# Layer 1 of a two-layer transformer: the opening stage's order of work on five queues, and the experts' products in one-pass float32r parts

## What is computed

```python
# end of layer 0 and opening of layer 1
h = jnp.tanh(jnp.einsum('tbi,oi->tbo', x, wo) + c_final @ uo.T + bo)   # z and cu hold the two summands
x = x + h
q = _layernorm(x, axis=-1) @ W_q.T + b_q
# experts of layer 1: E = 8, K = 2, hidden width 1024
h = jax.nn.gelu(jnp.einsum('ecd,edh->ech', buf, W1) + b1[:, None, :], approximate=False)
y = jnp.einsum('ech,ehd->ecd', h, W2) + b2[:, None, :]
```

## Time and profile before

| what | value |
|---|---|
| median of 3 runs | 6165.45 us (6163.56 to 6171.82) |
| the profiled execution, its own time | 6167.23 us |
| its span in the trace | 6165.5 us |
| mean granted TensorE clock | 0.91 |
| open_full, first DMA issue to the next stage's first | 1574.1 to 1814.5 us |
| experts, first DMA issue to the next stage's first | 4946.2 to 5977.5 us |

### The profile page before, as it was taken

One profiled execution on the slowest core, in us unless ns is written; L12 is line 12 of the kernel. 1 busy time (PEld: TensorE's weight loads), 2 busy tenths in 40 slices (PEclk: granted clock), 3 DMA queues, 4 the chain that ended last, 5 costly groups with the idle time before them and its releaser, 6 DMA issues. The chain is left out here.

```text
span 6165.5 us, 88753 instructions
## 1 busy us (share of the span) xinstructions
PE 5124.5 (83%) x27631; PEld 2717.2 (44%) x27632; DVE 3176.9 (52%) x6296; ACT 2503.8 (41%) x3173; POOL 1018.8 (17%) x786
## 2 busy tenths in 40 slices
PE   6778996699458999999999999999964089999970
PEld 3435664444224444443444444444343056666650
DVE  4556763211337888887888788888734000000013
ACT  1223552112114777776776677777620011111110
POOL 3440002311330000000000000000023700000016
PEclk8888998899778999999999999999876589999985
DMA  6445665700565333333333333333154421111115
GB/s 216 121 119 156 164 164 164 217 24 24 141 174 78 61 62 61 67 67 66 67 67 67 55 51 62 62 67 57 28 159 149 139 69 65 52 52 49 56 58 183
DMA packets 363364, 579.30 MB, mean 94 GB/s; under 512 B 56576, under 2 KB 258751, under 8 KB 360816
## 3 DMA queue, kind: packets, MB, share of 16 engines
q1 hardware_dynamic: 344976, 523.46, 35.7%
q0 software_dynamic: 14768, 50.51, 2.3%
q10 hardware_dynamic: 3264, 0.79, 0.1%
HBM read 297.72 MB, written 197.24 MB: 80 GB/s over the span
## 5 line engine op out<-in xcount | busy, mean ns | idle before, releaser
L1180 DVE TENSOR_REDUCE full_peak<-full_item 128x1 f32<-128x512 f32 (+2 forms) x3392 | 2036.2, 655 | 481.0 <-PE full_item L1247 475.4
L1150 ACT ACTIVATE full_prob<-full_score 128x1024 f32<-128x1024 f32 (+1 forms) x1792 | 1649.9, 960 | 659.9 <-PE full_score L1258 653.6
L1247 PE MATMUL full_item<-full_kst,full_qst 49*128 49x512 f32 (+1 forms) x4096 | 1205.2, 407 | 55.3 <-DVE full_peak L1180 23.8
L1258 PE MATMUL full_score<-full_qst,full_kst 51*128 51x512 f32 (+1 forms) x3328 | 1112.8, 448 | 17.3 <-ACT full_prob L1150 11.9
L1258 PEld LDWEIGHTS full_score<-full_qst,full_kst 51*128 51x128 f32 (+1 forms) x3328 | 481.1, 183 | 932.2 <-ACT full_prob L1150 600.6
L1272 PE MATMUL full_value<-full_prob,full_vaug 128*17 128x512 f32 x6656 | 887.0, 605 | 0.8 <-ACT full_raw L1137 0.7
L1247 PEld LDWEIGHTS full_item<-full_kst,full_qst 49*128 49x128 f32 x4096 | 630.5, 189 | 200.3 <-DVE full_peak L1180 129.4
L2069 ACT ACTIVATE moe_hT<-moe_hbank,moe_b 128x512 f32<-128x512 f32 (+1 forms) x320 | 199.4, 623 | 806.6 <-PE moe_hbank L2124 802.1
L2136 PE MATMUL moe_ybank<-moe_w,moe_hT 128*128 128x256 f32 x2176 | 485.1, 384 | 5.2 <-ACT moe_hT L2069 5.2
L2124 PE MATMUL moe_hbank<-moe_xT,moe_w 128*128 128x512 f32 (+1 forms) x1280 | 477.5, 531 | 6.4 <-DMA moe_b<-in_b 6.4
L2136 PEld LDWEIGHTS moe_ybank<-moe_w,moe_hT 128*128 128x128 f32 x2176 | 414.7, 192 | 67.3 <-issue 6.0
(11 more groups left out here) (207 smaller groups left out, 5282.2 us busy)
## 6 DMA issues: line engine op xcount, KB each, us to landing
full_kst<-full_high SPq DMA_DIRECT2D x256, 200.1 KB
full_ctxT<-in_ctxT SPq DMA_DIRECT2D x16, 1601.0 KB, 9.1
full_kst<-full_low SPq DMA_DIRECT2D x128, 200.1 KB
win_qst<-scratch_q SPq DMA_DIRECT2D x384, 64.0 KB, 2.6
full_qst<-scratch_q SPq DMA_DIRECT2D x384, 64.0 KB
scratch_xbuf<-ctxp_zero POOLq DMA_DIRECT2D x17, 1024.0 KB
scratch_attn<-win_raw SPq DMA_DIRECT2D x64, 256.0 KB, 2.1
scratch_q<-open_parts SPq DMA_DIRECT2D x128, 128.0 KB, 2.3
```

Source lines behind the costliest of these rows:

```text
L1150: nc.scalar.activation(prob[h][(s.par * PAIRS + t) % 2][0:rows, 0:banks, :], score[u % 2][0:rows, 0:banks, :], ACT.Exp, scale=SCALE).then_ ...
L1180: nc.vector.tensor_reduce(peak[s.par][:, hq:hq + len(qts), c], src, AX, ALU.max).then_inc(item_read, 1)
L1247: ins = nc.tensor.matmul(ps[:, at:at + z - a], qst[s.slot][rows, h // 2, qt * P:(qt + 1) * P].bitcast(F32R), kst[s.slot][rows, h // 2, a:z ...
L1258: ins = nc.tensor.matmul(score[u % 2][0:z - a, kt % 2, :], kst[s.slot][rows, h // 2, a:z].bitcast(F32R), qst[s.slot][rows, h // 2, :].bitc ...
```

## The change

In open_full: z, x1 and x2 get four buffers and semaphores of their own, and SP loads four batches ahead. The loops are written out. POOL adds cu two batches ahead (the z adds of 0 and 1 first; then for each n: the power, the z add of n+2, the low parts of n-1). ACT takes over the bias (`whole`) from DVE, and runs tanh of n+1, the copies and the bias reads of n. DVE runs for each n: the add, the statistics, the high parts of n-1, the centring of n. A pair of q stores becomes one, four stores a batch.

In experts: every operand of the two products is split into a high part (low 12 bits masked off) and a low part (the difference), both of type float32r, and each product becomes high by high, high by low and low by high. The hidden block takes 3 matmuls for each of its two halves. In the output rows the high part of h multiplies W2's high and low parts side by side (512 columns, halves of one PSUM bank), and the low part of h multiplies W2's high part (256 columns). DVE splits the weights of the next expert in eight pieces (three in chunk 1, three in chunk 2, two in chunk 3; those of expert 0 ahead of everything), the turned rows out of PSUM, and the hidden blocks; ACT makes the float32r copy of the hidden block's high part; DVE adds the two halves of an output bank and the bias, in two instructions for each tile. Rows are loaded two chunks ahead, and the raw weights have one buffer.

```diff
@@ open_full
+    BUFS = 4
...
         @block.gpsimd
...
-            def early(n, par):
-                pool.wait_ge(loads_in[par], 32 + 16 * (n - par))
-                nc.gpsimd.tensor_tensor(z[par][:, :, :], z[par][:, :, :], cu[:, :, :], ALU.add).then_inc(pre_done, 1)
-                pool.wait_ge(var_done, n + 1)
-                nc.gpsimd.tensor_tensor(norm[3][:, :], norm[2][:, :], minus_half[:, :], ALU.pow).then_inc(rstd_done, 1)
...
+            add_state(0)
+            add_state(1)
+            for n in range(BATCH):
+                pool.wait_ge(var_done, n + 1)
+                nc.gpsimd.tensor_tensor(rstd[:, :], var_eps[:, :], minus_half[:, :], ALU.pow).then_inc(rstd_done, 1)
+                if n + 2 < BATCH:
+                    add_state(n + 2)
+                if n > 0:
+                    low_parts(n - 1)
+            low_parts(BATCH - 1)
...
         @block.scalar
...
+            def read_queries(n):
+                for c in range(KC):
+                    act.wait_ge(q_full, KC * n + c + 1)
+                    if n >= 2:
+                        act.wait_ge(low_done, KC * (n - 2) + c + 1)
+                    nc.scalar.activation(whole[n % 2][c][:, :], qbank[2 * (n % 2) + c][:, :], ACT.Identity,
+                                         bias=bq[:, c:c + 1]).then_inc(q_read, 1)
...
         @block.vector
...
+            for n in range(BATCH):
+                add(n)
+                measure(n)
+                if n > 0:
+                    high_parts(n - 1)
+                centre(n)
+            high_parts(BATCH - 1)
@@ experts, ACT
+            def high_hidden(n, c, k):
+                cols = (CHUNKS[c][1] - CHUNKS[c][0]) * P
+                act.wait_ge(h_cut_done, (n * NC + c) * HC + k + 1)
+                nc.scalar.copy(h_high[:, k, 0:cols], h_cut[k % RING][:, 0:cols]).then_inc(h_high_done, 1)
...
-                        nc.scalar.activation(hT[parity(par, c)][:, k, 0:cols], hbank[k % 4][:, 0:cols], ACT.Gelu,
+                        if not (isinstance(n, int) and n == 0 and c == 0 and k < RING):
+                            act.wait_ge(h_low_done, (n * NC + c) * HC + k + 1 - RING)
+                        nc.scalar.activation(h[k % RING][:, 0:cols], hbank[k % 4][:, 0:cols], ACT.Gelu,
                                              bias=b1[par][:, k:k + 1]).then_inc(h_read, 1)
+                        if k > 0:
+                            high_hidden(n, c, k - 1)
@@ experts, DVE
+            def split_weights(n, par, j):
+                raw, part, (high, high_part), (low, low_part) = piece(j)
+                if j == 0:
+                    dve.wait_ge(w_in[par], 32 * (n - par) + 64)
+                nc.vector.tensor_scalar(cut_of(j).bitcast(U32), raw[part].bitcast(U32), HIGH_BITS, None,
+                                        ALU.bitwise_and).then_inc(w_cut_done, 1)
+                dve.wait_ge(w_cut_done, PIECES * n + j + 1)
+                nc.vector.tensor_copy(high[par][high_part], cut_of(j)).then_inc(w_high_done, 1)
+                nc.vector.tensor_tensor(low[par][low_part], raw[part], cut_of(j), ALU.subtract).then_inc(w_low_done, 1)
...
+            def split_hidden(n, c, k):
...
+                nc.vector.tensor_scalar(h_cut[k % RING][:, 0:cols].bitcast(U32), h[k % RING][:, 0:cols].bitcast(U32), HIGH_BITS,
+                                        None, ALU.bitwise_and).then_inc(h_cut_done, 1)
+                dve.wait_ge(h_cut_done, (n * NC + c) * HC + k + 1)
+                nc.vector.tensor_tensor(h_low[:, k, 0:cols], h[k % RING][:, 0:cols], h_cut[k % RING][:, 0:cols],
+                                        ALU.subtract).then_inc(h_low_done, 1)
+
+            def read_rows(n, par, c, i):
...
+                nc.vector.tensor_tensor(y_part[bank][:, :], ybank[bank][:, 1, :], b2[par][:, :], ALU.add).then_inc(y_part_done, 1)
+                dve.wait_ge(y_part_done, number + 1)
+                nc.vector.tensor_tensor(y[pg][:, i, :], ybank[bank][:, 0, :], y_part[bank][:, :], ALU.add).then_inc(y_read, 1)
...
                 for c, (a, z) in enumerate(CHUNKS):
+                    for k in range(HC):
+                        split_hidden(n, c, k)
                     if not (last and c == NC - 1):
                         read_turned(*following(n, par, c))
...
+                    if not last:
+                        for j in PIECES_IN.get(c, ()):
+                            split_weights(n + 1, 1 - par, j)
+                    at_least(dve, y_out[parity(par, c)], before(n, par, c))
+                    for i in range(z - a):
+                        read_rows(n, par, c, i)
@@ experts, PE
+            def hidden(n, par, c, k):
...
+                for kc in range(KC):
+                    high, low = (t[par][:, kc, k * P:(k + 1) * P] for t in (w1_high, w1_low))
+                    nc.tensor.matmul(out, high, x_high[pg][:, kc, 0:cols], start=(kc == 0), stop=False)
+                    nc.tensor.matmul(out, high, x_low[pg][:, kc, 0:cols], start=False, stop=False)
+                    ins = nc.tensor.matmul(out, low, x_high[pg][:, kc, 0:cols], start=False, stop=(kc == KC - 1))
+                ins.then_inc(h_full, 1)
+
+            def rows(n, par, c, i):
+                bank = ybank[(par + CHUNKS[c][0] + i) % 2]
+                pe.wait_ge(y_read, NY * n + CHUNKS[c][0] + i + 2 * NY - 1)
+                for hc in range(HC):
+                    if i == 0:
+                        pe.wait_ge(h_high_done, (n * NC + c) * HC + hc + 1)
+                        pe.wait_ge(h_low_done, (n * NC + c) * HC + hc + 1)
+                    nc.tensor.matmul(bank[:, :, :], h_high[:, hc, i * P:(i + 1) * P], w2_both[par][:, hc, :, :],
+                                     start=(hc == 0), stop=False, skip_group_check=True)
+                    ins = nc.tensor.matmul(bank[:, 0, :], h_low[:, hc, i * P:(i + 1) * P], w2_both[par][:, hc, 0, :],
+                                           start=False, stop=(hc == HC - 1), skip_group_check=True)
+                ins.then_inc(y_full, 1)
```

More of the change, by code:

```diff
@@ L1707, in _ @@
             sp.dma_start(ident[:, :], d["ident"]).then_inc(const_in, 16)
[L1709 to L1723, removed]
-            passes_two_ahead(sp, BATCH, loads, stores)
+            for n in range(1, BUFS):
+                loads(n)
+            for n in range(BATCH):
+                store_x2(n)
+                if n + BUFS < BATCH:
+                    loads(n + BUFS)
+                if n > 0:
+                    store_parts(n - 1)
+            store_parts(BATCH - 1)
+            for i in range(BUFS):
+                sp.wait_ge(x2_out[i], 16 * BATCH // BUFS)
             for i in range(2):
-                sp.wait_ge(x2_out[i], 8 * BATCH)
-                sp.wait_ge(parts_out[i], 64 * BATCH)
+                sp.wait_ge(parts_out[i], 64 * BATCH // 2)
         @block.gpsimd
@@ L1775, in late @@
-            def late(n, par):
-                if not (isinstance(n, int) and n < 2):
-                    dve.wait_ge(low_done, KC * (n - 1))
-                for c in range(KC):
-                    dve.wait_ge(q_full, 2 * n + c + 1)
-                    nc.vector.tensor_scalar(whole[par][c][:, :], qbank[2 * par + c][:, :], bq[:, c:c + 1], None,
-                                            ALU.add).then_inc(q_read, 1)
-                stored(dve, parts_out, n, par, 128)
-                for c in range(KC):
-                    dve.wait_ge(q_read, 2 * n + c + 5)
-                    nc.vector.tensor_scalar(parts[par][c][:, 0, :].bitcast(U32), whole[par][c][:, :].bitcast(U32),
-                                            HIGH_BITS, None, ALU.bitwise_and).then_inc(high_done, 1)
@@ new lines, in centre, with high_parts @@
+            def centre(n):
+                dve.wait_ge(rstd_done, n + 1)
+                if n >= 2:
+                    dve.wait_ge(t_full, KC * (n - 1))
+                for i in range(QT):
+                    ins = nc.vector.tensor_scalar(xn[n % 2][:, i, :], x2[n % BUFS][:, i, :], mv[:, i, 0:1], rstd[:, i:i + 1],
+                                                  ALU.subtract, ALU.mult)
+                ins.then_inc(xn_done, 1)
+            def high_parts(n):
+                for c in range(KC):
+                    dve.wait_ge(q_read, KC * n + c + 1)
+                    if n >= 2:
+                        dve.wait_ge(parts_out[n % 2], 64 * (n // 2))
+                    nc.vector.tensor_scalar(parts[n % 2][c][:, 0, :].bitcast(U32), whole[n % 2][c][:, :].bitcast(U32),
+                                            HIGH_BITS, None, ALU.bitwise_and).then_inc(high_done, 1)
@@ L1807, in one @@
                     ins.then_inc(q_full, 1)
-            passes(pe, BATCH, one)
 def route(nc, d):
@@ L1974, in experts @@
     HC = HID // P
-    YJOBS = [(c, j) for c, (a, z) in enumerate(CHUNKS) for j in range(-(-(z - a) // 2))]
-    NY = len(YJOBS)
+    NY = SLOT_TILES
+    RING = 4
+    PIECES = 8
+    PIECES_IN = {1: (0, 1, 2), 2: (3, 4, 5), 3: (6, 7)}
```

(2 more changed lines are left out.)

223 lines of the change are left out of this document (140 added, 83 removed).

## The result

The kernel after takes **6025.14 us** (median of 3 runs, 6021.98 to 6031.51), the kernel before 6165.45: a ratio of 0.9772, with a 95% interval of 0.9750 to 0.9794. The profiled execution took 6021.98 us, its span is 6020.2, its mean granted clock 0.907 (before 0.91). Forecast were 6003 us, 5935 to 6080. The 140 us gained are 22 fewer than the forecast has.

What follows compares the result with a forecast made beforehand. It took experts to be bound by PE's matmuls and open_full by a loop through all engines. Gains of 121 us (experts) and 41 us (open_full) from 6167.2 gave 6005 us profiled, 6003 as median; range 5935 to 6080.

Steps and rivals of the forecast that it cites:

- open_full: The opening stage: z add leaves the loop, a turn falls from 13.7 to 11.0 us, a gain of 41 us.
- The price of a float32r matmul: Experts, PE: one pass, 0.215 us for 512 columns where float32 needs 0.86; 10.3 us for a chunk's hidden layer.
- The stalls: Experts: PE waits for DVE before output tile 2, 4.05 us each in chunks 1 and 2, 1.0 in chunk 3.
- The clock: Experts: both 4.05 us stalls of an expert cause a fall of PE's clock, 14 x 2.6 = 36 us.
- The start: Experts: eight weight pieces and turned rows come before PE's first hidden matmul, making it 13.9 us later.
- 109 to 112: Experts: sign that the forecast holds, an expert's period near 109 to 112 us.
- rival 1: Experts: DVE or ACT is the bound, copies into float32r cost 0.69 us, not 0.30; time 6060 us, chance 0.20.
- Rivals 3 and 4: Experts, slower: no one-pass float32r on the full array, 6565 us, chance 0.05; ACT reloads tables, 6800 us, chance 0.03.
- break-even: Experts: the slower case of float32r without one pass decides from about 0.30 us for a 512-column matmul on.
- Rival 2: open_full gains nothing, since port, clock and DMAs close the loop again at 13.7 us; 6044 us, chance 0.06.
- The floor of 9.75 us from the DMAs: open_full: 13.74 us at a share of 0.71 is 9.75 us of all DMA engines; no turn is shorter.
- The prediction's sum by it: open_full: POOL's 5.94 us a batch, two masks and the centring can't overlap, 8.2 us, DVE's add on top.

Runs made afterwards that it cites:

- experiment 3: Kernel after, with each of DVE's weight pieces in experts moved behind the read of an output tile instead of all ahead of the first: 5933.64 us, ratio 0.9629.
- experiment 5: Kernel after, with DVE's centring of n placed ahead of the high parts of n-1 in open_full: 5990.37 us in one run.
- experiment 10: Kernel after with the changes of experiment 3 and experiment 5, plus POOL's low parts ahead of its z add in open_full: 5902.87 us, ratio 0.9568.
- experiment 4: Kernel after, with the weight pieces spread two in each of chunks 0 to 3, still ahead of the output tiles: 6027.18 us in one run.

## Why the prediction was right, and where its sum was off

The sign, the range and the mechanisms held: both gains are there, each by the path that the prediction names. The forecast's gain was 162 us and the profiled execution shows 145 (6167.2 - 6022.0). But 12 of these come from full attention, which the prediction costed at no change since stages run one after another; that they made the sum look better is luck. Without them it is 133, so the two terms of the forecast are 29 us too kind. Point by point:

- **The price of a float32r matmul was mis-sized: 0.229 us for 512 columns instead of 0.215.** This is the largest error. A hidden chunk takes 11.0 us instead of 10.3, a pair of output matmuls 0.353 instead of 0.332. That is 0.7 + 0.65 in each of four large chunks, some 5.3 us an expert, 43 in all. The earlier trace rows held a hint: I fitted the shortest records (383 ns) where the median of line 1247 is 396, and the records of the kernel after have means of 393 to 395. These 10 to 13 ns are most of the 14 missing ones. It was no more than a hint, since the median of line 1258 is 443.
- **The stalls were there,** two an expert, ended by DVE's second addition: 3.5 us instead of 4.05 (14 x 0.55 = 8 us less), partly since PE comes to the third tile later with slower pairs. In chunk 3 they are 0.75 us, where 1.0 was forecast (2 us less).
- **The clock:** 14 falls, as forecast. By experiment 3 they cost 32 us at most (half of 65), forecast 36.
- **The start:** the first hidden matmul comes 25.4 us after the stage's first instruction (4926.13 - 4900.76), before 13.1: 12.3 us more, forecast 13.9.
- Together 43 - 8 - 2 - 4 - 2 = 27 us too kind for experts, and 21 were measured (121 - 99.6). The 6 between them are not taken apart in full. The largest piece is the transposes, forecast at 0.93 us a chunk: they took 0.79, and 0.14 in chunk 3, some 9 us less. Against it stands, among others, the first hidden chunk, which began at the lower level and took 12.9 us instead of 11.0. An expert's period was 114.6 us, outside the 109 to 112 given as a sign.
- **DVE and ACT are not the bound** (rival 1): the copy into float32r has a duration of 0.427 us and a step of 0.34, within my 0.30 to 0.42, and hidden blocks come 1.37 us apart at PE's pace. The groups by form of the kernel after, which answer to the earlier trace rows:

```profile
L2200 DVE TENSOR_TENSOR moe_h_low<-moe_h,moe_h_cut 128x512 fp32r<-128x512 f32 x256 | 177.3, 693 | 8.8
L2158 ACT ACTIVATE moe_h<-moe_hbank,moe_b 128x512 f32<-128x512 f32 x256 | 176.4, 689 | 451.5 <-PE moe_hbank L2251 449.9
L2148 ACT CAST moe_h_high<-moe_h_cut 128x512 fp32r<-128x512 f32 x256 | 156.2, 612 | 0.0
...
L2176 DVE CAST moe_w_high<-moe_w_cut 128x512 fp32r<-128x512 f32 x32 | 13.7, 427 | 1.1
```

- **Rivals 3 and 4 are void.** On the full array 512 columns are one record each, 0.229 us apart, and the break-even was at 0.30. ACT alternates between Gelu and the cast with one table load in the whole stage; this agrees with what the Trainium skill (ScalarE: Activation LUTs, Table sets: the hidden batching unit) says of copies.
- **open_full:** a turn of 11.46 us where I took 11.0, and a mean turn of 13.60 before where I took 13.7: 15 x 0.56 is the 8 us missing. The causes were right: there are 14 falls of the clock in the 15 turns (the matmuls of the turn shown take 5.11 us), and the centring takes 2.33 us beside a low part. Experiment 5 confirms the loop, by cutting it. The DMA share was 0.78, and not near 0.9. Rival 2, no gain here, did not come.
- **The floor of 9.75 us from the DMAs was no floor.** Time times share (13.74 x 0.71) was read as work that the DMAs can't do faster; experiment 5 has turns of 9.07 us, with no byte less (178 GB/s for 240.4 us before, 255 for 168.3 there). In the stretch of the earlier trace rows the same product is 9.75 before, 8.9 after, 8.5 in experiment 5 (0.94 x 9.07) and 8.6 in experiment 10: it shrinks as the loop gets tighter. So the share counts as busy what can still be packed closer. At shares of 0.94 and 0.97 there is little left to pack; whether the DMAs would be the next bound below some 8.5 us was not tested. The forecast did not rest on it, but the lower end of the range did, and "the prediction is wrong if a turn falls below 9.8" would have been a false alarm.
- **The lock between DVE and POOL.** The timelines show four cases: the first centring instruction takes 2.43 us and ends with the z add, four take 3.40; beside one low part 2.33; beside nothing 1.38 (before, and experiment 10); and DVE's add of batch 0 takes 2.20 us instead of 1.21 while POOL adds cu. Which of the two waits changes: in experiment 10 the low parts take 3.74 us instead of 2 x 1.27. The Trainium skill (SBUF — State Buffer, Who interferes with whom) says that the one excludes the other for the whole instruction, and the trace agrees in each of these. The prediction's sum by it, 8.2 us without DVE's add and 9.4 with it, lies on both sides of the 8.85 us of experiment 10. That kernel comes near to such a sum, but the sum is of durations, and instructions that follow each other on DVE overlap by some 0.08 us in the trace (four of 0.41 us end after 1.38).

## What to carry to other kernels

When an engine gets more work ahead of the reads that free another engine's buffers, the order in its queue counts before the amount: the same 610 us on DVE cost 86 us more or less by where the pieces stood. Don't price a new instruction by the fastest of its relatives in the trace; look at the spread, and give it as a range. After a stall is moved off one queue, walk the loop again on every engine: the 2 us taken from the centring came back on POOL within the same turn. And compare the stages that nobody edited, in all kernels: here 12 us of the gain stood in one of them, and only the kernels with one half of the change showed which half they came with.

## What was not expected of the hardware

- The clock fell at waits of 2.1 us on PE that came once in a chunk (experiment 4: 17 of 21), not only at waits of 3.5 us. In the kernel after, 14 waits of 3.5 us go with 14 falls. Without these waits (experiment 3) there are no falls inside the experts.
- The surplus of a float32r matmul vanishes at the lower level: a pair of 512 and 256 columns takes 0.64 us there, which is 768 columns at 1.2 GHz, but 0.353 instead of 0.320 at the higher level. So what it waits for does not seem to be counted in PE's own cycles. What it is stays open.
- DVE writes float32r at the price of its other 4-byte types: 0.427 us for a copy of 512 elements inside SBUF (a mask 0.418 in the earlier trace rows), 0.69 for a subtraction.
